# Gated cross-attention with a routed expert layer: loads, query groups, key chunks and the last two tiles rearranged

## What is computed

```python
x = x + tanh(g_xattn[0]) * xattn(layernorm(x), ctx, ctx)   # x (8,112,256), ctx (8,375,192)
#   q = xn @ Wq + bq ; k = ctx @ Wk + bk ; v = ctx @ Wv + bv ; 16 heads of 16
#   out = softmax(q k^T / 4) v ; out @ Wo + bo
x = x + tanh(g_ffn[0]) * ffn(layernorm(x))
#   top-1 routing of 896 tokens to 8 experts with 112 places each, in token order;
#   a token without a place gets nothing:  gate * (x @ W[e].T + b[e])
```

## Time and profile before

| | |
|---|---|
| median of 3 runs | 225.27 us (225.04 to 226.06) |
| profiled execution | 226.61 us, its span 224.8 us |
| mean granted TensorE clock | 0.922 |
| busy | PE 184.9 us (82%), PEld 111.7, DVE 123.7, ACT 91.5, POOL 94.3 |
| HBM | 10.03 MB read, 5.29 MB written |

### The profile page before, as it was taken

One profiled execution on the slowest core, in us unless ns is written; L12 is line 12 of the kernel. 1 busy time (PEld: TensorE's weight loads), 2 busy tenths in 40 slices (PEclk: granted clock), 3 DMA queues, 4 the chain that ended last, 5 costly groups with the idle time before them and its releaser, 6 DMA issues.

```text
span 224.8 us, 4335 instructions
## 1 busy us (share of the span) xinstructions
PE 184.9 (82%) x1692; PEld 111.7 (50%) x1692; DVE 123.7 (55%) x292; ACT 91.5 (41%) x200; POOL 94.3 (42%) x145
## 2 busy tenths in 40 slices
PE   0866869743999899899899989989989896479990
PEld 0342426412556466557556646646656563257640
DVE  7037465563454855754764675485585436254651
ACT  0262243231374365456527527544636654021200
POOL 5632639779245056038037235413022553103730
PEclk9999599995699999999999999999999998556998
DMA  6968049999940910840660490180351233560110
GB/s 187 264 156 169 0 107 291 226 238 294 291 139 16 224 65 5 191 109 3 142 162 0 100 203 3 40 171 0 94 146 57 69 113 116 155 175 28 57 51 20
DMA packets 17660, 27.40 MB, mean 122 GB/s; under 512 B 4007, under 2 KB 12817, under 8 KB 17272
## 3 DMA queue, kind: packets, MB, share of 16 engines
q1 hardware_dynamic: 15176, 23.82, 41.6%
q0 software_dynamic: 944, 2.28, 3.3%
q10 hardware_dynamic: 1520, 1.03, 1.9%
HBM read 10.03 MB, written 5.29 MB: 68 GB/s over the span
## 4 chain that ended last, share of the span: by engine, by line
PE 66%; DVE 13%; DMA 8%; POOL 5%; ACT 2%; issue 2%; ACTq 1%; SPq 1%; DVEq 0%
PE stp L476 14%; PE pv L491 12%; PE sc L465 8%; PE misc L522 4%; PE stp L407 4%; DMA bv_sb<-in_bv 4%; DVE nmax L809 4%; PE pj L423 3%; PE pj L439 3%; PE misc L580 2%; DVE pvT L816 2%; DMA k<-parts_k 2%; DMA q<-mrows 2%; PE pj L444 2%; PE pv L580 2%
## 5 line engine op out<-in xcount | busy, mean ns | idle before, releaser
L809 DVE TENSOR_REDUCE nmax<-sc 112x1 f32<-112x375 f32 x128 | 68.2, 543 | 54.6 <-PE sc L465 53.8
L733 ACT ACTIVATE prob<-stp 125x448 f32<-125x448 f32 x96 | 52.2, 544 | 61.2 <-PE stp L476 60.8
L465 PE MATMUL sc<-k,q 128*112 128x375 bf16 x128 | 41.8, 343 | 9.1 <-DVE nmax L809 6.7
L476 PE MATMUL stp<-q,k 128*125 128x112 bf16 x384 | 42.8, 236 | 3.2 <-DMA q<-mrows 3.2
L491 PE MATMUL pv<-prob,v_sb 125*32 125x112 f32 x768 | 38.7, 273 | 2.1 <-issue 1.3
L476 PEld LDWEIGHTS stp<-q,k 128*125 128x125 bf16 x384 | 30.3, 140 | 20.1 <-issue 16.5
L491 PEld LDWEIGHTS pv<-prob,v_sb 125*32 125x32 f32 x768 | 15.4, 108 | 23.6 <-ACT prob L733 10.1
L1000 POOL TENSOR_SCALAR ve<-mv 112x1 f32<-112x1 f32 x8 | 1.9, 233 | 57.4 <-DVE mv L838 57.4
L465 PEld LDWEIGHTS sc<-k,q 128*112 128x112 bf16 x128 | 17.2, 135 | 16.4 <-DVE nmax L809 11.4
L423 PE MATMUL pj<-ctx_sb,wk_sb 128*128 128x375 f32 x32 | 15.4, 580 | 7.8 <-DMA ctx_sb<-in_ctx 7.8
L1017 POOL TENSOR_TENSOR kf<-kf,parts_k 128x375 f32<-128x375 f32 x14 | 12.6, 899 | 19.1 <-ACT kf L677 19.1
(11 more groups left out here) (125 smaller groups left out, 240.7 us busy)
## 6 DMA issues: line engine op xcount, KB each, us to landing
k<-parts_k SPq DMA_DIRECT2D x48, 187.5 KB, 3.8
ctx_sb<-in_ctx SPq DMA_DIRECT2D x2, 1125.0 KB, 7.6
early<-in_wT SPq DMA_DIRECT2D x8, 256.0 KB, 4.3
slots<-empty SPq DMA_DIRECT2D x8, 224.9 KB, 4.6
ctx_sb<-slots SPq DMA_DIRECT2D x8, 224.9 KB, 4.5
q<-parts_q SPq DMA_DIRECT2D x6, 224.0 KB, 3.7
q<-parts_q SPq DMA_DIRECT2D x6, 168.0 KB, 3.7
k<-in_be SPq DMA_DIRECT2D x1, 896.0 KB, 5.1
```

The costliest lines, as they stand in the source:

```text
L465: pe.matmul(sc[h % 2][0:NQ, 0:NK], q_heads(b)[:, h, :], k6[:, b % KR, h, :], start=True, stop=True).then_inc(s_sc, 1)
L476: mm = pe.matmul(stp[n % 2][0:KN, j * NQ:(j + 1) * NQ], k6[:, b % KR, h, c * KN:(c + 1) * KN], q_heads(b)[:, h, :], start=True, stop=True)
L733: nc.scalar.activation(prob[0:KN, n % 3, :], stp[n % 2][0:KN, 0:4 * NQ], ACT.Exp, scale=SCALE).then_inc(s_p, 1)
L809: nc.vector.tensor_reduce(nmax[:, b % 2, h:h + 1], sc[h % 2][0:NQ, 0:NK], axis=AX.X, op=ALU.max, negate=True).then_inc(s_max, 1)
```

## The change

1. Loads: ctx of tile 0 goes first on SP, x of tile 0, wk, one tile for the three biases, and wq on ACT; all other weights and gates move to SP. x comes in pieces of tiles 0, 1 to 2 and 3 to 7. ctx of tiles 2 to 4 is issued by ACT.
2. Query groups are tiles 0, 1 to 2, 3 to 5, 6 to 7. K of tile 1 is projected, split and laid ahead of the loop, in front of most constants; the loop starts at step 0. Long fills on POOL are cut into pieces.
3. Chunks are 128, 128 and 119 keys. `scores_T` always loads 128 columns of `k6`, which has 16 more columns for it; the columns over 119 are not used.
4. `normalise_pv` becomes three pieces at steps 30, 31, 32. `through_wo` goes to 33, `add_x` to 34, the layer norm to 35, `turn_xn2` to 37, `logits` to 38; `split_max`, `turn_max` and the transfer of the maxima come a step earlier (12, 13, 14).
5. Tiles 6 and 7 both go through all experts. Only six tiles are scattered. `dense` of tile 6 stands between the pieces of tile 7's attention tail.
6. Nine matmuls of zeros, 512 columns each, stand ahead of TensorE's first real work, and a first `Tanh` on zeros loads ACT's table.

```diff
-NCH = 3
-KN = NK // NCH
+CHUNKS = [(0, 128), (128, 128), (256, NK - 256)]
-V_EARLY = -10
-SPLITMAX_AT, MAXT_AT, MROW_AT = 13, 14, 15
+V_EARLY = -11
+SPLITMAX_AT, MAXT_AT, MROW_AT = 12, 13, 14
 T_AT, PV_AT = 17, 18
-NORM_AT, WO_AT, ADD_AT = 30, 31, 32
-LN_AT, X2T_AT, LG_AT = 33, 35, 36
-FIRST, LAST = -4, TURN * (B - 1) + LG_AT
-QG = ((0, 1), (1, 5), (5, 8))
-R0, R1, R2 = (0, 6), (6, 7), (7, 8)
-ROUTE0_AT, PLACE0_AT, ASSIGN0_AT = 97, 98, 99
-ROUTE1_AT, PLACE1_AT, ASSIGN1_AT = 109, 110, 111
-SCAT0_AT = (100, 101, 102, 106, 107, 108)
+NORM_AT, WO_AT, ADD_AT = (30, 31, 32), 33, 34
+LN_AT, X2T_AT, LG_AT = 35, 37, 38
+END = TURN * (B - 1) + PV_AT + UNITS
+WARM = 9
+QG = ((0, 1), (1, 3), (3, 6), (6, 8))
+GATHERED = 6
+ROUTE0_AT, PLACE0_AT, ASSIGN0_AT = 99, 100, 101
+ROUTE1_AT, PLACE1_AT, SHARE1_AT = 111, 112, 113
+SCAT_AT = (102, 103, 104, 105, 106, 107)
...
-        k6_flat = sb("k6", [128, KR, H * NK], BF16)
+        k6_flat = sb("k6", [128, KR, H * NK + 16], BF16)
...
-            sp.dma_start(wk_sb[:, :, :], wk).then_inc(s_wk, 16)
             load_ctx(0, 0, 1)
-            sp.dma_start(x_sb[:, 1:5, :], x[:, 1:5, :]).then_inc(s_x[1], 16)
+            sp.dma_start(x_sb[:, 1:3, :], x[:, 1:3, :]).then_inc(s_x[1], 16)
             load_ctx(1, 1, 2)
-            sp.dma_start(x_sb[:, 5:B, :], x[:, 5:B, :]).then_inc(s_x[2], 16)
+            sp.dma_start(x_sb[:, 3:B, :], x[:, 3:B, :]).then_inc(s_x[2], 16)
             lay_k(0)
             lay_q(0)
+            lay_k(1)
+            lay_q(1)
...
-            sp.wait_ge(s_scat, 16 * (B - 1))
+            sp.wait_ge(s_scat, 16 * GATHERED)
...
                 for j in range(4):
                     h = 4 * g + j
-                    mm = pe.matmul(stp[n % 2][0:KN, j * NQ:(j + 1) * NQ],
-                                   k6[:, b % KR, h, c * KN:(c + 1) * KN], q_heads(b)[:, h, :],
+                    k0 = h * NK + CHUNKS[c][0]
+                    mm = pe.matmul(stp[n % 2][:, j * NQ:(j + 1) * NQ],
+                                   k6_flat[:, b % KR, k0:k0 + 128], q_heads(b)[:, h, :],
                                    start=True, stop=True)
...
             def turn_xn2(b):
                 pe.wait_ge(s_xn2, b + 1)
+                pe.wait_ge(s_mrows, min(b + 3, B))
...
+            pe.wait_ge(s_qzero[0], 1)
+            for _ in range(WARM):
+                pe.matmul(sc[0][:, :], q6[:, 0:128], q6[:, 0:512], start=True, stop=True)
+            pe.wait_ge(s_ident, 1)
+            turn_xn(0)
             pe.wait_ge(s_wk, 16)
             for n in range(K_STEPS):
                 project_k(0, n)
...
             pe.wait_ge(s_wT, 16 * E)
+            turn_share(0)
+            dense(0, 0)
+            through_wo(B - 1)
+            choose_bias(0)
+            dense(0, 1)
+            turn_xn2(B - 1)
             turn_xin(0)
-            places(2, *R2)
+            logits(B - 1)
+            dense(0, 2)
+            places(2, B - 1, B)
+            dense(0, 3)
+            turn_xin(1)
...
+            pe.wait_ge(s_beTe, 2)
+            for p in range(4):
+                dense(1, p)
...
-            normalise(0)
-            dve.wait_ge(s_bias, 48)
-            k_rest(0, 0)
-            k_rest(0, 1)
-            q_rest(0, 0)
-            q_rest(0, 1)
+            normalise(0, 1)
+            nc.vector.memset(k6_flat[:, 1, :].bitcast(F32), TWO_ONES).then_inc(s_kones[1], 1)
             dve.wait_ge(s_x[1], 16)
-            statistics(1, 5)
-            normalise(1)
+            statistics(1, 3)
+            normalise(1, 3)
+            dve.wait_ge(s_bias, 16)
+            for m in range(2):
+                k_rest(0, m)
+            for m in range(2):
+                q_rest(0, m)
             dve.wait_ge(s_x[2], 16)
-            statistics(5, 8)
-            normalise(2)
+            statistics(3, 6)
+            normalise(3, 6)
+            for m in range(2):
+                q_rest(1, m)
+            statistics(6, 8)
+            normalise(6, 8)
...
                 if found := at(s, SPLITMAX_AT, 1):
                     split_max(found[0])
                 for m in range(2):
-                    if (found := at(s, KSPLIT_AT[m], 1)) and found[0] > 0:
+                    if (found := at(s, KSPLIT_AT[m], 1)) and found[0] > 1:
                         k_split(found[0], m)
...
                 if found := at(s, LN_AT, 1):
                     rstd_2(found[0])
-                    if found[0] < R1[0]:
+                    if found[0] < GATHERED:
                         normalise_2(found[0])
```

More of the change, by code:

```diff
@@ L295, in group_of @@
         def group_of(b):
-            return 0 if b < QG[1][0] else 1 if b < QG[2][0] else 2
+            return [g for g, (lo, hi) in enumerate(QG) if lo <= b < hi][0]
         def q_heads(b):
@@ L438, in project_v @@
                     pe.wait_ge(s_kf, 2 * (newest - 1) + n + 1)
-                    pe.matmul(pj[n][0:KN, 0:D], keys(n, slice(0, 128), 0), wv_sb[:, 0, :],
+                    pe.matmul(pj[n][:, half:half + D], keys(n, slice(0, 128), 0), wv_sb[:, 0, :],
                               start=True, stop=False)
@@ L447, in project_v @@
                     for c in range(2):
-                        pe.matmul(pj[c][0:KN, D:D + 128], keys(2, slice(0, 128), 0),
-                                  wv_sb[:, 0, c * 128:(c + 1) * 128], start=True, stop=False)
+                        pe.matmul(pj[c][0:kn, 0:half], keys(2, slice(0, 128), 0),
+                                  wv_sb[:, 0, c * half:(c + 1) * half], start=True, stop=False)
                 if n == 4:
@@ L925, in _ @@
                         take_max(found[0], h)
-                if s in (7, 8):
-                    q_rest(2, s - 7)
-                if s == 10:
+                if s in (5, 9):
+                    for m in range(2):
+                        q_rest(2 if s == 5 else 3, m)
+                if s == 11:
                     dve.wait_ge(s_tanh, 1)
@@ L970, in _ @@
                                                ALU.mult, ALU.add).then_inc(s_res, 1)
-            dve.wait_ge(s_share, 1)
-            dve.wait_ge(s_beT, 1)
-            link(nc.vector.tensor_tensor(last[:, :], pv[0:NQ, 0:D], rows[:, b, X1:X1 + D], ALU.add))
-            banks = (pj[0], pj[1], stp[0], stp[1])
-            for e in range(E):
-                if e % 2 == 0:
-                    dve.wait_ge(s_dense, e // 2 + 1)
-                ins = nc.vector.scalar_tensor_tensor(
-                    last[:, :], banks[e // 2][0:NQ, (e % 2) * D:(e % 2 + 1) * D], share[:, e:e + 1],
-                    last[:, :], ALU.mult, ALU.add)
-                if e < E - 1:
-                    link(ins)
-                else:
-                    ins.then_inc(s_last, 1)
+                if e == 3:
+                    take_bias(1)
+            for p in range(4):
+                add_dense(1, p)
         @block.gpsimd
@@ L1057, in _ @@
                 q_lo(0, m)
[L1058 removed]
             rstd(2)
[L1061 to L1064 removed]
+            for m in range(2):
+                k_split(1, m)
+            rstd(3)
+            for m in range(2):
+                q_lo(1, m)
+            ones_in_k(2)
+            zeros_in_q(2)
+            zeros_in_q(3)
+            nc.gpsimd.memset(v_sb[:, :, :, HD:32], 1.0).then_inc(s_vones, 1)
             def more_constants():
```

428 lines of the change are left out of this document (244 added, 184 removed).

## The result

The changed kernel takes 256.69 us (median of 4, 255.83 to 257.96) where the kernel before takes 225.36 (225.04 to 226.06): a ratio of 1.139, 95% interval 1.133 to 1.145. The prediction was 227.0 with a range of 211.5 to 234. The profiled execution has a span of 254.9 us against 224.8, at a mean granted clock of 0.866 against 0.922. In the experiments the kernel before took anything from 220.8 to 229.4 us, by chip and by execution, so a ratio depends on which of these it is taken to, and totals of different chips can't be compared more closely than some 2%.

A forecast was written before the change was run, and what follows sets the result against it. The prediction took TensorE to bound the loop, busy 17.11 of 18.10 us. Head -6, loop +10 and tail -2.3 summed to +1.7 us on 225.27, giving 227.0 us, range 211.5 to 234.

The forecast's parts named there:

- The head: Start to turn_max of tile 0: from 49.5 to 43.5 us, a gain of 6, bounds 3 and 12.
- VectorE then has to finish the normalisation of tiles 6 and 7: Head: this work, waiting for POOL's rstd, sets the first maximum at about 25.4 us, 4.2 us sooner.
- The keys and queries of tile 0 laid 1 to 1.5 us sooner: Head: follows from k_rest at about 12.3 us against 12.90, the bias no longer ending the first K copy's wait.
- The twelve steps behind the first maximum: Head, up to turn_max of tile 0: gain the 1.2 us wait for ctx, carry a second query group of 2.1 us.
- The loop, the added wait: Four turns: layer norm behind k_split delays split_max; TensorE waits 3.45 us, plus 0.5 for mrows; turns 20.9 against 18.16 us.
- Rival B: Loop: POOL is not late, so four times 3.6 us come off, giving 212.6 us; chance 0.30.
- rival C: Loop: the four 3.45 us waits let the clock fall; two falls of 3 to 5 us, 235 us; chance 0.14.
- A: Whole kernel: the forecast itself, 227.0 us, spread 223 to 231; chance 0.40.
- The loads of 128 columns: scores_T: weight loads stop setting the pace, 0.045 us per unit, 4 us over the loop, bounds +0.7 and -10.
- D: scores_T: loads of 128 columns quick enough to gain 8 us instead of 4, giving 222.5 us; chance 0.16.
- The normalisation in pieces: Loop: the score waits about 0.15 us for its maximum instead of 0.77; 0.8 us per turn, bounds 0.5 and 1.4.
- The tail: Last probs_v to last sum: 29.4 us instead of 31.7, a gain of 2.3, experts at 1.06 us each.

The follow-up runs named there:

- e1: Changed kernel, but GpSimd waits for VectorE's last normalisation of x before its fills of k6 (third buffer), q6 (groups 2 and 3) and v; 255.28 us.
- e13: Kernel of e9 with ACT's load of ctx of tiles 2 to 4 issued behind its first Tanh; 220.05 us.
- e7: Kernel before with part 4 of the change alone; 256.26 us, ratio 1.158.
- e2: Changed kernel with maxima, normalisation, output product, layer norm and logits set back to the steps of the kernel before; 228.96 us.
- e11: Changed kernel with 14 unread products on TensorE ahead of turn_max's wait for the split maxima, tiles 2 to 7; 250.37 us.
- e6: Kernel before with one edit: scores_T loads 128 columns of k6 instead of 125, chunks staying 125 keys; 218.79 us, ratio 0.989.
- e3: Changed kernel with the edits of both e1 and e2; 221.75 us, ratio 0.973.
- e14: The same kernel as e3, run again on another chip; 218.51 us, ratio 0.969.
- e4: Changed kernel, fills held back, normalisation at 30, 30, 31, layer norm at 34, maxima at 13, 14, 15; 217.56 us, ratio 0.983.
- e9: The same kernel as e4, run again on another chip; 217.73 us, ratio 0.980.
- e5: Changed kernel with GpSimd taking the second layer norm ahead of k_split within its step; 257.03 us.

## Why the prediction was wrong

**The head (predicted -6 us, measured +8.2).** Four steps failed.

- "VectorE then has to finish the normalisation of tiles 6 and 7": the work was named, its price taken as that of an undisturbed instruction. What stood beside it on GpSimd, the fills cut into pieces, was put at nothing without a reason. It took 8.62 us instead of 1.30. Of the 14.2 us by which the head missed, 7.4 are this (e1, shown).
- "The keys and queries of tile 0 laid 1 to 1.5 us sooner": they came later. TensorE now turns x of tile 0 ahead of K and waits for its normalisation, so K starts at 9.17 where it was 6.59; SP starts laying K at 14.06 instead of 13.35 and the queries at 18.40 instead of 17.34. I had followed the wait for the bias that went, and not the order of TensorE's own queue. Of the 2.6 us by which K starts later, 1.3 are by the trace again fills: the normalisation of tile 0 took 1.70 us beside them instead of 0.41. No run moved these fills, so this isn't tested, and it is part of the head in e1 and e13 too.
- "SP issues its moved loads [...] before it has anything to lay, so they cost nothing": true of SP's, but the load that moved to ACT, 1125 KB at 17.3 us, was not in the sum. It makes each transfer of the queries take 3 us longer to land (e13, shown). Together with VectorE this puts the first maximum at 28.3 in e1, and at 27.3 in e13, instead of 25.4.
- The twelve steps behind the first maximum: 22.0 us in e1 instead of 18.1. `turn_max` of tile 0 waits 2.5 us for GpSimd, which splits the last queries (1.22), then K (2.35) and only then the maxima (1.06). This is the same queue that I had counted in the loop and forgot in the head. By the traces the half clock in the first of these steps takes the rest; neither was tested by itself.

The bounds of the head (3 to 12 us gained) held no case in which it loses, although the part adds work to two engines ahead of the first maximum.

**The loop, the added wait (predicted 3.45 + 0.5, measured 3.13 + 0.44).** Right, with its queue, its place and its number: four times, as predicted. With the wait filled a turn takes 21.08 us for the predicted 20.9. Rival B (GpSimd is not late) is out. That part 4 alone brings it is shown by e7, and that it goes with the step by e2.

**The clock.** This is the step that failed in the loop. It stood as rival C, "A stretch of one or two slices [...] at half speed", two falls, 8 us, with a chance of 0.14, as if it were another case than A. It is the same case: here the fall comes in every turn that has the wait. Between first and last `turn_max` the sum gave 124.2 + 9 = 133.2 us; e11 takes 135.3, the kernel after 143.7. e11 less the 4.6 us of products that fill no wait is 130.7: the sum was 2.5 us too long by itself, and the clock costs 13 us of the 143.7 (8.4 if e11 is taken as it stands). Of the remaining 4 us of the loop's miss 3.5 lie behind the last `turn_max`: 20.5 us to the last `probs_v`, for 17.0 predicted, with the 10.2 us at 1.2 GHz that begin at 204.36. What brings that fall on stays open. A range up to 234 couldn't hold what C in every turn comes to.

**The loads of 128 columns (predicted 4 us over the loop, bounds +0.7 and -10).** e6 gives 4.9 from first to last `turn_max`. The estimate was right, with pairs 49 ns apart as it had them; D (8 us) is out.

**The normalisation in pieces (predicted 0.8 us per turn).** In the kernel after the weight load of the scores behind it waits 0.27 us, where it waited 0.90 before. But e3 and e14, with it in one step, have turns of 17.52 us, and e4 and e9, with two pieces and a later layer norm, are shorter by 0.25 on average. By these it was worth a third of what I took. Some of that may be the later layer norm; three pieces alone were not tried.

**The tail (predicted 29.4 us from the last `probs_v` to the last sum).** Measured 29.5 (221.87 to 251.35), with 1.03 us for each product of the experts from the first and the clock at 1.0. Right, with some luck: the fall at the end of the loop was over 7.3 us before the tail began. In e1, e5 and e11 it reaches into the tail, and from the last `probs_v` to the end of the span they take 35.2, 34.9 and 34.6 us, where the kernel after takes 33.1.

**The zeros.** "If the clock falls again before K, they bring nothing either": right, and without them nothing is lost either.

**Slips in the sums.** 119.16 to 121.56 is 2.40 us and not 2.35, 128/125 of the pace over 96 units is +0.5 us and not +0.7, and the terms of the loop (+11, -1, -1, +1.5) add up to 10.5, written as 10. None of them changes a reading.

The loads and the tail, priced right, gain 4.9 and 2.2 us. With the fills held back and part 4 undone (e3, e14) or its layer norm put one step later than before instead of two (e4, e9), the ratios of the change are 0.969 to 0.983, where as it stands it is 14% slower.

## What to carry to other kernels

A wait of some 3 us on TensorE in each turn of a loop should be priced as the wait and a fall of the clock behind it (here 3 us more), once per turn, and not as a rare second case. Follow each queue by what stands in it at that step, ahead of the loop too: a layer norm one step later did no harm, and two steps later, with the maxima a step sooner, it cost 29 us of a loop of 124. When an engine gets fills or a large load is moved, look at what the engine or the queue beside it is doing at that time, since here the fills fell into a time in which GpSimd had nothing else to do, and held up its neighbour.
